# Both edge loops of a graph network written out in a row, with constants for addresses and semaphore counts

## What is computed

```python
# layer 0: attention over edges, then a feed-forward part, both normalised
m      = leaky_relu(xl[src] + xr[dst] + edge_attr @ W_e, 0.2)
logits = einsum('eho,ho->eh', m, att)                # 8 heads of 16
exl    = exp(logits - segment_max(logits, dst)[dst])
out    = segment_sum(xl[src] * exl / segment_sum(exl, dst)[dst], dst)
h      = layer_norm(x + out);  x2 = layer_norm(h + gelu(h @ W1) @ W2)
x      = layernorm(x + x2)
# layer 1: a convolution over the same edges
h   = gelu(gelu(edge_attr_8 @ W_mlp1) @ W_mlp2)      # 64 wide
w   = h @ Wp                                          # 4 x 32 weights an edge
mid = products of w, feat[src] and edge_attr_4        # 256 wide
n   = segment_sum(mid, dst);  x = layernorm(x + mix(self(x), n @ W2))
```

## Time and profile before

| | us |
|---|---|
| median of 3 runs (lowest, highest) | 5867.4 (5851.1, 5890.8) |
| span of the profiled execution | 5855.7 |
| the median less the span, what lies around it | 11.7 |
| TensorE, VectorE, ScalarE, GpSimd busy | 3865.5, 3222.6, 1837.0, 3371.9 |
| attention, first to last use of line 1049 | 151.1 to 3025.5 |
| convolution, first to last use of line 1516 | 3169.4 to 5786.7 |

### The profile page before, as it was taken

The page is one execution under the profiler, slowest core; times in us unless marked ns, Lnnn a source line. Parts: engine busy times, 40 slices in busy tenths (PEclk is TensorE's granted clock), DMA queues, the critical chain, the costliest instruction groups (busy, mean ns, idle before and its releaser), DMA issues. The chain is left out here.

```text
span 5855.7 us, 86247 instructions
## 1 busy us (share of the span) xinstructions
PE 3865.5 (66%) x15016; PEld 2606.4 (45%) x15016; DVE 3222.6 (55%) x10018; ACT 1837.0 (31%) x5130; POOL 3371.9 (58%) x3264
## 2 busy tenths in 40 slices
PE   2666666666666666666664775786776677776676
PEld 2334444434444444444443554554554455454454
DVE  3344454545444554454554675675666556675665
ACT  1234334344334344334452221221222122222221
POOL 3455555555555555555525776666777666767763
PEclk6878878888888888888876897887888778887787
DMA  5433333333333333333311111111111111111111
GB/s 151 120 103 100 100 99 98 93 101 104 96 100 100 100 98 101 98 102 99 101 51 54 44 44 43 43 42 43 44 43 44 41 42 44 44 42 45 43 42 41
DMA packets 395313, 430.82 MB, mean 74 GB/s; under 512 B 195187, under 2 KB 286839, under 8 KB 394888
## 3 DMA queue, kind: packets, MB, share of 16 engines
q0 software_dynamic: 103168, 211.49, 13.8%
q1 hardware_dynamic: 291560, 216.64, 13.7%
q10 hardware_dynamic: 288, 0.04, 0.0%
HBM read 411.18 MB, written 16.65 MB: 73 GB/s over the span
## 5 line engine op out<-in xcount | busy, mean ns | idle before, releaser
L171 POOL DMA_INDIRECT ring_rows<-xl,ring_idx x1612 | 1537.0, 953 | 1444.3 <-DVE attn_msg L1043 898.6
L218 POOL DMA_INDIRECT ahead_rows<-feat,ahead_idx x1612 | 1796.1, 1114 | 834.1 <-issue 513.5
L878 PE MATMUL attn_sums_ps<-attn_msg,attn_onehot 128*128 128x136 f32 x3224 | 601.9, 344 | 934.8 <-DVE c_acc_attn L984 541.8
L1433 PE MATMUL conv_sums_ps<-conv_vals,conv_onehot 128*128 128x256 f32 x3224 | 924.6, 436 | 157.6 <-issue 95.9
L878 PEld LDWEIGHTS attn_sums_ps<-attn_msg,attn_onehot 128*128 128x128 f32 x3224 | 524.3, 240 | 987.6 <-DVE c_acc_attn L984 742.6
L1464 ACT ACTIVATE conv_scaled<-conv_w_ps,c_xT 128x64 f32<-128x64 f32 x1612 | 373.4, 314 | 1643.7 <-remote 729.0
L1433 PEld LDWEIGHTS conv_sums_ps<-conv_vals,conv_onehot 128*128 128x128 f32 x3224 | 654.5, 214 | 414.1 <-issue 310.1
L1440 PE MATMUL conv_w_ps<-c_Wp,conv_hid 128*128 128x256 f32 x1612 | 505.7, 444 | 484.1 <-ACT conv_hid L1470 266.5
L929 ACT ACTIVATE attn_fifth<-attn_pre_ps,c_b_r 128x512 f32<-128x512 f32 x403 | 275.0, 683 | 1505.4 <-remote 953.7
L1049 DVE SCALAR_TENSOR_TENSOR attn_leaky<-attn_pre_ps,c_b_r,attn_fifth 128x512 f32<-128x512 f32 x403 | 301.1, 747 | 743.5 <-ACT attn_fifth L929 599.1
L1489 DVE TENSOR_SCALAR conv_onehot<-c_iota,c_dst_pos 128x128 f32<-128x128 f32 x1612 | 357.1, 297 | 509.0 <-remote 374.6
(11 more groups left out here) (214 smaller groups left out, 4795.7 us busy)
## 6 DMA issues: line engine op xcount, KB each, us to landing
c_xT<-in_attrT SPq DMA_DIRECT2D x403, 256.0 KB
attn_rel<-rel_group SPq DMA_DIRECT2D x403, 126.0 KB
ring_rows<-xl,ring_idx POOLq DMA_INDIRECT x1612
ahead_rows<-feat,ahead_idx POOLq DMA_INDIRECT x1612
ahead_radial<-in_radialT SPq DMA_DIRECT2D x806, 8.0 KB
attn_xr_win<-xr_parts SPq DMA_DIRECT2D x403, 31.5 KB
attn_limit<-limit SPq DMA_DIRECT2D x403, 16.0 KB
ahead_idx<-in_src_tiles SPq DMA_DIRECT2D x403, 2.0 KB
```

The source lines that it names most:

```text
L171: pool.indirect_dma_start(self.rows[:, b, t, :], None, self.q["xl"][:, :], bass.IndirectOffsetOnAxis(ap=self.idx[:, s.slot(2), j * TG + t: ...
L218: pool.indirect_dma_start(self.rows[:, k.slot(U), t, :], None, self.q["feat"][:, :], bass.IndirectOffsetOnAxis(ap=self.idx[b][:, t:t + 1], ...
L878: last = nc.tensor.matmul(to, onehot[:, g.slot(2), t, :], msg[:, g.slot(2), t, :, :].rearrange("p h o -> p (h o)"), start=wins > 1 or t == ...
L1433: last = nc.tensor.matmul(to, onehot[:, g.slot(2), t, :], vals[:, g.slot(2), t, :], start=wins > 1 or t == 0, stop=wins > 1 or t == TG - 1)
```

## The change

`steps` gets a flag `written_out`. With it the turns are unrolled in Python: `body` is called for every step of every turn, with a Python number for `i`. So that `body` still does in these steps what it did in the loop (the job on nodes, the choice of PSUM halves), `Step` gets `turns`, which says that a step belongs to the turns, and each test for "`i` is not a number" becomes a test of `turns`. The flag is set for both edge loops of the narrow path on all five engines; the wide path keeps its loops, and so do `update_nodes` and `finish_nodes`.

```diff
 class Step:
-    def __init__(self, at, i=0, stride=U):
-        self.at, self.i, self.stride = at, i, stride
+    def __init__(self, at, i=0, stride=U, turns=False):
+        self.at, self.i, self.stride, self.turns = at, i, stride, turns
...
     def index(self, scale=1, plus=0):
         base = self.at * scale + plus
-        return base if isinstance(self.i, int) else self.i * (self.stride * scale) + base
+        return self.i * (self.stride * scale) + base if self.turns else base
...
-def steps(eng, total, peel, unroll, tail, body, last=0):
+def steps(eng, total, peel, unroll, tail, body, last=0, written_out=False):
     for k in range(peel):
         body(Step(k, 0, unroll), lambda lag, k=k: 0 <= k - lag < total)
-    if total - last > peel:
-        with eng.Fori(0, (total - last - peel) // unroll) as i:
+    turns = (total - last - peel) // unroll
+    if written_out:
+        for i in range(turns):
             for u in range(unroll):
-                body(Step(peel + u, i, unroll), lambda lag: True)
+                body(Step(peel + u, i, unroll, True), lambda lag: True)
+    elif turns > 0:
+        with eng.Fori(0, turns) as i:
+            for u in range(unroll):
+                body(Step(peel + u, i, unroll, True), lambda lag: True)
...
-                steps(sp, G, PEEL, U, 0, body, END)
+                steps(sp, G, PEEL, U, 0, body, END, wins == 1)
...
-            steps(pool, G, PEEL, U, 0, body, END)
+            steps(pool, G, PEEL, U, 0, body, END, True)
...
-                steps(pe, G, PEEL, U, TAIL, body, END)
+                steps(pe, G, PEEL, U, TAIL, body, END, wins == 1)
...
-            steps(act, G, PEEL, U, TAIL, body, END)
+            steps(act, G, PEEL, U, TAIL, body, END, True)
...
-                steps(dve, G, PEEL, U, TAIL, body, END)
+                steps(dve, G, PEEL, U, TAIL, body, END, wins == 1)
...
-            steps(sp, G, PEEL, U, 0, body)
+            steps(sp, G, PEEL, U, 0, body, written_out=True)
...
-                steps(pe, G, PEEL, U, TAIL, body)
+                steps(pe, G, PEEL, U, TAIL, body, written_out=wins == 1)
...
-            steps(act, G, PEEL, U, TAIL, body)
+            steps(act, G, PEEL, U, TAIL, body, written_out=True)
...
-                steps(dve, G, PEEL, U, TAIL, body)
+                steps(dve, G, PEEL, U, TAIL, body, written_out=wins == 1)
```

More of the change, by code:

```diff
@@ L225, in place @@
     s, j = WHERE[g.at]
-    return Step(s, g.i, SPAN // B), j, SIZES[s]
+    return Step(s, g.i, SPAN // B, g.turns), j, SIZES[s]
 def lines_in_slot(s):
     base = 16 * SAME_SLOT[s.at]
-    return base if isinstance(s.i, int) else s.i * (16 * B) + base
+    return s.i * (16 * B) + base if s.turns else base
 def messages(k, later, live):
-    if not isinstance(k.i, int):
+    if k.turns:
         return [k.back(STEADY + later)]
@@ L572, in one_slot @@
         def one_slot(g):
-            return not isinstance(g.i, int) or LOOP_FROM - STEADY - 2 <= g.at < G - AFTER_LOOP - STEADY - 1
+            return g.turns or LOOP_FROM - STEADY - 2 <= g.at < G - AFTER_LOOP - STEADY - 1
         def sums_slot(g):
@@ L601, in job_of @@
         def job_of(k):
-            return Step(0, k.i, 1)
+            return Step(0, k.i, 1, True)
         def job_nodes(table, job):
@@ L806, in body @@
                                  .partition_broadcast(H).rearrange("p a n -> p (a n)")).then_inc(limit_loaded[s.slot(2)], 16)
-                    if wins == 1 and not isinstance(k.i, int):
+                    if wins == 1 and k.turns:
                         job_on_sp(sp, job_of(k), k.at - PEEL)
                 load_x(sp, Step(0))
-                steps(sp, G, PEEL, U, 0, body, END)
+                steps(sp, G, PEEL, U, 0, body, END, wins == 1)
                 if wins > 1:
@@ L813, in run @@
                         for u in range(U):
-                            job_on_sp(sp, Step(0, i, 1), u)
+                            job_on_sp(sp, Step(0, i, 1, True), u)
                 sp.wait_ge(x_loaded, 16 * (JOBS + 1))
@@ L823, in body @@
             def body(k, live):
-                if not live(0) or (isinstance(k.i, int) and k.at < EARLY):
+                if not live(0) or (not k.turns and k.at < EARLY):
                     return
-                if not isinstance(k.i, int) or k.at >= NX:
+                if k.turns or k.at >= NX:
                     pool.wait_ge(msg_ready, k.back(NX).uses())
@@ L893, in body @@
                         nc.tensor.transpose(turn_ps[:, s.slot(2), DROPS:DROPS + H], drop_row[:, :], ident[0:H, 0:H]).then_inc(max_turns, 1)
-                    if wins == 1 and isinstance(k.i, int) and k.at == G + 3:
+                    if wins == 1 and not k.turns and k.at == G + 3:
                         pe.sem_inc(hidden_ready, FC * JOBS)
-                    if not isinstance(k.i, int):
+                    if k.turns:
                         u, c = k.at - PEEL, k.at - PEEL - U_HIDDEN
@@ L910, in run @@
                         for u in range(U):
[L911 removed]
+                            job_on_pe(pe, AFTER, Step(0, i, 1, True), Step(JOBS, i, 1, True), u)
             by_width(pe, sb["narrow"], run)
@@ L1128, in body @@
                     sp.dma_start(x_rows[:, k.slot(4), :, :], nodes("x_pad", k)).then_inc(x_loaded[k.slot(4)], 16)
-                if isinstance(k.i, int) and k.at == 3:
+                if not k.turns and k.at == 3:
                     for n in range(CONV_ND):
@@ L1402, in body @@
             def body(k, live):
-                if not live(0) or (isinstance(k.i, int) and k.at < ND):
+                if not live(0) or (not k.turns and k.at < ND):
                     return
@@ L1413, in body @@
             def body(k, live):
-                if not live(0) or (isinstance(k.i, int) and k.at < AHEAD):
+                if not live(0) or (not k.turns and k.at < AHEAD):
                     return
-                if not isinstance(k.i, int) or k.at >= NX:
+                if k.turns or k.at >= NX:
                     pool.wait_ge(vals_ready, k.back(NX).uses())
@@ L1419, in body @@
                 ahead.gather(pool, k)
-            steps(pool, G, PEEL, U, 0, body)
+            steps(pool, G, PEEL, U, 0, body, written_out=True)
         @block.tensor
```

7 lines of the change are left out of this document (3 added, 4 removed).

## The result

The changed kernel takes 5707.8 us (median of 4 runs, 5679.8 to 5720.5) beside 5872.6 us for the kernel before: a ratio of 0.971, with an interval of 0.968 to 0.975. The forecast was 5677 us in a range of 5420 to 5835. The total fits; its two terms do not. The attention was to give 70 us and gave some 196; the convolution was to give 120 us and lost some 20.

A forecast was written before the change was run, and what follows sets the result against it. No firm bound; GpSimd's issues (5.0 us a step) came nearest in both loops. Convolution 120 us (110 constants, 10 turns) plus attention 70 us made 190 us off 5867.4: 5677 us, range 5420 to 5835.

The forecast's parts named there:

- The bound: In both loops GpSimd is nearest to a bound: four indirect DMAs of 1.25 us, 5.0 us a step.
- Part 1, the turns: Removing turns gains 42 us in the attention (14 DVE stalls of 3.0 us) and 10 us in the convolution.
- Part 2, constants in the convolution: Fewer instructions, mainly on DVE and SP, remove a third of GpSimd's 340 us of waiting: 110 us.
- my ends of 10 and 340: Lower and upper end, in us, of the convolution's whole gain, which was put at 120 us.
- the crawl: Convolution stretches where GpSimd issues without pause, sequencer instructions take 0.70 us instead of 0.04, and a DVE step takes 21.7 us.
- Part 3, the attention: In the attention, 42 us from turns plus 2 us a turn (28) from fewer register operations: 70 us.
- The written-out stretch ahead of the loop: Last 24 attention steps before its loop, already constants: 157.6 us against 175.5 a turn, giving the upper end, 250 us.
- Rival A, the fetch: Written-out convolution must stream some 275 instruction packets; 69 stalls of 3 us lose 206 us: 6003 us, chance 0.08.
- Rival B: GpSimd's pace and TensorE's late messages decide everywhere; only the turns' 52 us are gained: 5815 us, chance 0.20.
- Rival C: The crawl mostly vanishes with fewer instructions; convolution loses 340 us, attention 250 us: 5277 us, chance 0.14.
- What would show it: List of signs in the new profile, for both loops, that would prove the forecast right or wrong.
- an unchanged 3.98 us step: Sign: DVE's full-pace convolution step, which has no gap to close, still takes 3.98 us after the change.

The follow-up runs named there:

- experiment 3: Both edge loops written out with register operations kept, attention in 2 turns of 168 steps, convolution in 7 of 56, against the kernel before: 5890.7 us, ratio 1.006.
- experiment 2: Only the convolution written out, the attention left a loop, against the kernel before: 5885.5 us beside 5856.9, ratio 1.005.
- Experiment 4: The full change, but DVE's attention program stays a loop of 14 turns, against the kernel before: 5804.3 us, ratio 0.992.
- 5: The full change, with GpSimd in the convolution also held within 2 steps of TensorE, against the kernel before: 4349.2 us beside 4319.6, ratio 1.009.
- 10: The full change with GpSimd held within 2 steps of TensorE in the convolution, run a second time, against the kernel before: 4362.1 us, ratio 1.010.
- 12: The full change, with GpSimd held within 2 steps of TensorE in the convolution and 3 in the attention, against the kernel before: 4374.7 us, ratio 1.013.
- experiment 7: The kernel before, with only DVE's attention program written out and everything else left as loops: 4317.9 us beside 4319.6, ratio 1.000.

## Why the prediction was right in sum and wrong in its parts

The sum fits by luck. It was to be 120 + 70 = 190 us; by the two lengths it was -19 + 196 = 177 us. The convolution fell short of its term by 139 us and the attention went over its own by 126, and the two errors cancel.

*The bound.* Right that GpSimd's 1.25 us an issue is the floor and that the first chip's loops miss it by messages and slow instructions. The second chip shows the floor itself, 5.02 us a step.

*Part 1, the turns: 52 us.* Wrong, as far as experiment 3 shows: it removes 12 of 14 and 42 of 49 turns, the attention's stalls all but vanish from the waits, and no time is gained. The step that failed is "POOL is then mostly waiting for DVE, so it lies on the path": that DVE pauses while GpSimd waits for DVE doesn't make the pause count, if the messages that come after it are late for another reason. That this is why is argued, not shown.

*Part 2, constants in the convolution: 110 us.* Wrong in size and sign: a loss of 19 us in the changed kernel and 28 in experiment 2, outside my ends of 10 and 340. The step that failed is the one from "32 x 0.70 = 22.4 us, which is the crawl's step" to "10 x 0.70 = 7 us of DVE's 21.7". The agreement was chance: right behind the 21.7 us DVE stood another 11.18 us for a message of TensorE, which the count leaves out. DVE's slow instructions fell from 329 to 30 us of idle time, and the crawling steps did not shrink to 15 us: those over 12 us went from 18.7 to 20.9 us on average. What DVE no longer spent on them it waited for TensorE and ScalarE (405 to 755 us). The forecast had said so itself ("TensorE, which tells late as well, loses least") and still let DVE's count set the term.

*Part 3, the attention: 70 us.* The mechanism of the range holds, the value was mis-sized. I had put 42 us on turns, worth 0, and 28 us on constants, worth 196: 14 us a turn where I took 2. The written-out stretch ahead of the loop, whose upper end was 250 us, was the better guide: 160 us per 24 steps now (2678.0 / 402 x 24), 157.6 there. I set it aside since a turn carries 19 us more of DVE's busy time; but DVE idles half of the attention, and added busy work there costs little. That it costs little is argued. What the waits show of the 196 us: 107 us less waiting of DVE for ScalarE, 38 less for unnamed messages, and 32 less "issue". I had priced only what DVE's own instructions take and nothing for messages that come sooner.

*Rival A, the fetch.* Refuted at its size of 206 us: the convolution lost 19. It does fetch now, 170 packets in 2540 us where I had expected some 275 and where the loop had none (3060 to 5600 us):

```profile
q8 instruction: 54, 0.88, 0.1%
q14 instruction: 116, 0.95, 0.1%
```

DVE's idle time with no wait ("issue") in that stretch is 56 us in all, where the loop had 400. On the second chip, where every stall of GpSimd would show in the total, the written-out convolution is longer by the length of its issues alone. Whether fetches have a part in the 19 to 28 us lost on the first chip is open. The Trainium skill, "Runtime: NRT & Kernel Launch", Instruction fetch mechanics, ties a stall to a taken branch out of the held pages; straight-line fetches at which no stall shows agree with that, and experiment 3 adds that taking away most of the stalls behind such branches gained nothing.

*Rival B* (no change, since GpSimd's pace and late messages decide) fits the convolution's result, and its reason fits the waits; it was wrong for the attention. *Rival C*, the crawl mostly gone, did not happen through the change. It happened by going to another chip.

*What would show it.* Right: no stall every 24 steps, an unchanged 3.98 us step, packets all through. Wrong: the attention at about 170 us per 24 steps (160), the convolution at 6.2 to 6.3 us a step (6.56), its wait for indices clearly under 296 (334), a crawling step of 15.

*What stays open.* Why TensorE's messages come late, and register operations take 0.7 us, on one chip and not on the other. My forecast took GpSimd's unbroken issues for the cause. They are not enough: on the second chip GpSimd issues every 1.25 us from end to end and nothing crawls. That the crawl ends when GpSimd stops is read from ScalarE's start in one timeline (1.7 us, above), and DVE's start in the same crawl, 9.6 us before GpSimd stopped, speaks against it; the kernels made to test it, 5, 10 and 12, met the wrong chip. Nor is it shown why constants help the attention and not the convolution. Experiment 4 shows only that DVE's own loop undoes half of the gain. And it is not shown that the chip itself makes the difference: each chip was used in its own stretch of time, and what else ran beside the kernel isn't on record.

## What to carry to other kernels

A stall, or a row of slow instructions, counts only if the next thing that the engine waits for would have been there sooner: follow it to that wait before pricing it, and test the count (here: the same rows of code with the registers kept) before believing that a product of two numbers explains a duration. Constants in place of registers paid in the attention on the first chip. They paid nothing in its convolution, where late messages set the time, and nothing on the second chip, where one engine's pace did. And a gain that is made of waiting may belong to the chip: with the change the kernel is 2.9% faster in the result and 0.7% slower on the second chip, so measure on more than one before keeping it.

## What the runs showed of the hardware that I had not expected

This one-core kernel takes 5857 us on one chip and 4320 on two others, each steadily. The engines' instructions themselves are as long: DVE's leaky step has a median of 750 ns in experiment 3, on the first chip, and 751 in experiment 7, on the second. What differs is the waiting: register operations of 0.7 us, and TensorE's messages, 24 us late for DVE and 34 for ScalarE in the crawl above.

TensorE's granted clock follows. It reaches 1.00 (2.4 GHz) in the changed kernel's profile too, while the engines are at full pace, and is down at 0.50 (1.2 GHz) in the part of the crawl in which TensorE stands idle, from 3082.2 us on:

```profile
3030.00:3058.00 28.00, 27.98 (x117) 20.44 (x115) 28.00 (x100) 11.29 (x47) 23.73 (x15) 1.00 0.15 37
...
3096.00:3110.00 14.00, 0.00 (x0) 0.00 (x0) 3.89 (x13) 0.93 (x4) 7.54 (x8) 0.50 0.16 42
```

TensorE's eight products of a step took 3.78 us in the crawl and 1.99 at full pace, a difference of 1.8 us in a step of 25.5. So the mean of 0.81 (0.95 on the second chip) goes with the waiting, and in this crawl little of the waiting comes from it.

GpSimd's issue gets longer beside dense work of DVE: 2.42 us in place of 0.94 beside the full-pace step, on the changed kernel as before, and 977 ns on average in place of 959 when the other engines' instructions stand closer. The Trainium skill, "SBUF — State Buffer", Who interferes with whom, has DVE instructions with two inputs in SBUF contend with GpSimd instructions that read SBUF. The trace agrees that an issue gets longer beside DVE's work; which instruction holds it up was not tried.
